# Flamingo layer on one core: values ahead of scores, and the twelve transposes together, in each attention step

## What is computed

```python
# attention (scale = 1/sqrt(sqrt(64)))
x = layer_norm(ctx) ; l = layer_norm(_layernorm(x_in))
q = l @ Wq ; k, v = split(concatenate([x, l]) @ Wkv)
w = softmax((q * scale) @ (k * scale).T)         # 256 x 333 for each head
out = (w @ v).reshape(B, 256, 1024) @ Wo
x_in = x_in + tanh(g_xattn) * out
# then: x + tanh(g_ffn) * (routed experts, top 2 of 16, + a shared expert with a causal conv of 3 taps)
```

## Time and profile before

| | |
|---|---|
| median of 3 runs | 1342.59 us (1341.72 to 1343.8) |
| the profiled execution | 1342.28 us |
| its span, first to last instruction | 1340.5 us |
| TensorE busy | 1251.8 us, 93% |
| VectorE, GpSimd, ScalarE busy | 65%, 55%, 50% |
| mean granted clock of TensorE | 0.988 |

### The profile page before, as it was taken

How to read it: one execution, slowest core, us unless ns; L and a number is a source line. 1 busy time by engine, 2 the same in 40 slices (tenths; PEclk the granted TensorE clock), 3 DMA queues, 4 the chain that set the end, 5 groups by cost and what they waited for, 6 DMA issues and landing times.

```text
span 1340.5 us, 28196 instructions
## 1 busy us (share of the span) xinstructions
PE 1251.8 (93%) x8982; PEld 1018.9 (76%) x8982; DVE 877.1 (65%) x2646; ACT 665.2 (50%) x2022; POOL 739.4 (55%) x894
## 2 busy tenths in 40 slices
PE   1799999999999999999999999999999979999996
PEld 1687888878887878787878787888788867887774
DVE  4567667777776777777777776777776654444454
ACT  2455555455545455455454554555545545444443
POOL 1655555656565666566656655665665522444554
PEclk9999999999999999999999999999999989999998
DMA  4960000000000000000000000000000151445656
GB/s 128 287 181 4 4 1 4 17 4 17 4 18 5 17 4 18 5 17 4 18 6 17 8 13 6 17 11 9 10 9 9 52 149 39 121 127 169 206 177 205
DMA packets 61823, 70.90 MB, mean 53 GB/s; under 512 B 7056, under 2 KB 56160, under 8 KB 61664
## 3 DMA queue, kind: packets, MB, share of 16 engines
q1 hardware_dynamic: 54464, 49.96, 12.9%
q0 software_dynamic: 6912, 18.95, 4.0%
q10 hardware_dynamic: 288, 0.00, 0.0%
HBM read 35.19 MB, written 33.70 MB: 51 GB/s over the span
## 4 chain that ended last, share of the span: by engine, by line
PE 39%; POOL 28%; issue 23%; DVE 5%; DMA 3%; ACT 2%; POOLq 0%; SPq 0%; DVEq 0%; ACTq 0%
POOL probs L1107 19%; PE pj L1344 9%; PE st L560 6%; PE ov L1409 4%; PE st L1390 4%; PE st L1374 3%; POOL probs L1104 3%; POOL slots_x L977 3%; PE pj L513 3%; PE ov L579 3%; PE yb L1470 2%; PE st L550 2%; POOL rstd L1087 1%; DMA slots_x<-h_send,slot_i 1%; DVE PT L1328 1%
## 5 line engine op out<-in xcount | busy, mean ns | idle before, releaser
L1107 POOL TENSOR_SCALAR probs<-probs,inv_sum 128x333 f32<-128x333 f32 x384 | 425.4, 1123 | 0.0
L1157 ACT ACTIVATE probs<-st,neg_max 128x333 f32<-128x333 f32 x512 | 268.5, 537 | 270.9 <-DVE neg_max L1296 270.9
L1104 POOL TENSOR_TENSOR probs<-probs,inv_sum 128x333 f32<-128x333 f32 x128 | 94.7, 740 | 403.2 <-DVE inv_sum L1307 402.9
L1296 DVE TENSOR_REDUCE neg_max<-st 128x2 f32<-128x666 f32 x256 | 205.8, 845 | 133.0 <-PE st L1390 133.0
L1374 PE MATMUL st<-ident,probs 128*128 128x128 f32 (+1 forms) x1536 | 203.8, 272 | 1.1 <-POOL probs L1107 1.1
L1409 PE MATMUL ov<-PT,V 128*64 128x256 f32 (+1 forms) x1536 | 197.1, 392 | 0.0
L1374 PEld LDWEIGHTS st<-ident,probs 128*128 128x128 f32 (+1 forms) x1536 | 182.5, 143 | 17.7 <-POOL probs L1107 1.4
L1344 PE MATMUL pj<-wkv,lT 128*128 128x512 f32 (+1 forms) x576 | 158.4, 410 | 16.3 <-DVE Q_hl L1316 15.8
L1390 PE MATMUL st<-K_hl,Q_hl 64*128 64x334 f32 x1536 | 152.9, 331 | 18.3 <-issue 8.9
L1328 DVE COPY PT<-st 128x512 f32<-128x512 f32 x256 | 163.7, 681 | 0.7 <-PE st L1374 0.7
L1183 ACT ACTIVATE V<-pj 128x512 f32<-128x512 f32 (+1 forms) x96 | 57.2, 596 | 194.4 <-PE pj L1344 194.4
(11 more groups left out here) (174 smaller groups left out, 1729.4 us busy)
## 6 DMA issues: line engine op xcount, KB each, us to landing
slots_x<-zeros SPq DMA_DIRECT2D x10, 1032.0 KB, 13.2
V<-slots_x SPq DMA_DIRECT2D x80, 129.0 KB
yg<-routed_y SPq DMA_DIRECT2D x32, 256.0 KB
out<-X SPq DMA_DIRECT2D x32, 128.0 KB
stage<-in_L_xattn_Wkv SPq DMA_DIRECT2D x4, 512.0 KB, 4.0
X<-in_x SPq DMA_DIRECT2D x2, 1024.0 KB, 14.2
w_gu<-in_L_ffn_expert_gate_w SPq DMA_DIRECT2D x2, 960.0 KB, 9.2
w_gu<-in_L_ffn_expert_up_w SPq DMA_DIRECT2D x2, 960.0 KB, 10.2
```

The source lines that it names most:

```text
L1104: pool.tensor_tensor(probs[:, v, 0, 0:SKV], probs[:, v, 0, 0:SKV], inv_sum[:, v, 0:1].to_broadcast([P, SKV]), ALU.mult).then_inc(normed, 1)
L1107: pool.tensor_scalar(probs[:, v, i, 0:SKV], probs[:, v, i, 0:SKV], inv_sum[:, v, i:i + 1], None, ALU.mult).then_inc(normed, 1)
L1157: nc.scalar.activation(probs[:, v, i, 0:SKV], st_bank(i)[:, 0:SKV], ACT.Exp, bias=neg_max[:, v, i:i + 1], accum_out=sums[:, v, i:i + 1]).t ...
L1296: nc.vector.tensor_reduce(neg_max[:, v, 2 * i:2 * i + 2], st[i][:, :, 0:SKV], AX.X, ALU.max, negate=True).then_inc(maxed, 1)
```

## The change

TensorE: the products with values go ahead of the scores; the twelve transposes, before in two groups (eight ahead of V, four behind it), go together behind V and L in a step with V, ahead of the output projection, and behind the output projection in a step without V. ScalarE copies `ov` to `OT_hl` ahead of the exponentials, and VectorE takes the remainder of `OT_hl` ahead of the maxima (behind the add of a finished batch at p = 3). The routing products stay with the output projection. All waits are the same.

In the diff the blocks of `OT_hl` are shown at their new places only, and of TensorE's the new functions; its block of scores stands behind that of values. `project_out` holds the wait for `ot_lo`, the conv transposes, `route_tensor` and the output projection as they were.

```diff
@@ scalar, step @@
+            if has(LAG_AV):
+                m, v = PAIRS * bb + u - LAG_AV, (u - LAG_AV) % 2
+                act.wait_ge(ov_full, m + 1)
+                if known(m - 1):
+                    act.wait_ge(y_full, m - 1)
+                copy(OT_hl[:, v, 0, :], ov[:, 0:SQ], ACT.Copy).then_inc(ot_hi, 1)
             if has(LAG_S):
...
@@ vector, step @@
+            if has(LAG_AV):
+                m, v = PAIRS * bb + u - LAG_AV, (u - LAG_AV) % 2
+                dve.wait_ge(ot_hi, m + 1)
+                tt(OT_hl[:, v, 1, :], ov[:, 0:SQ], OT_hl[:, v, 0, :].bitcast(F32), ALU.subtract
+                   ).then_inc(ot_lo, 1)
             if has(LAG_S):
...
@@ tensor, step @@
-            if has(LAG_T):
-                pe.wait_ge(normed, 4 * (PAIRS * bb + u - LAG_T + 1))
-                turned(0)
-                turned(1)
             if p in V_STEPS and has(0):
...
-            if has(LAG_T):
-                turned(2)
             if p in L_STEPS and exists(b + 1) and exists(b):
                 transposes(bb, u // PAIRS + 1, L_STEPS[p])
...
+            def turn_probs():
+                if has(LAG_T):
+                    pe.wait_ge(normed, 4 * (PAIRS * bb + u - LAG_T + 1))
+                    turned(0)
+                    turned(1)
+                    turned(2)
+
+            def project_out():
+...
+
+            if p in V_STEPS:
+                turn_probs()
+                project_out()
+            else:
+                project_out()
+                turn_probs()
```

More of the change, by code:

```diff
@@ L1159, in step @@
                                          accum_out=sums[:, v, i:i + 1]).then_inc(exped, 1)
[L1160 to L1165, removed]
             if has(0):
@@ L1307, in step @@
                 nc.vector.reciprocal(inv_sum[:, v, :], sums[:, v, :]).then_inc(inv_ready, 1)
[L1308 to L1312, removed]
             if has(0):
@@ L1375, in turned @@
                 last.then_inc(pt_full, 1)
[L1377 to L1392, removed]
             if has(LAG_AV):
@@ L1411, in step @@
                 last.then_inc(ov_full, 1)
+            if has(LAG_S):
+                m, r = PAIRS * bb + u - LAG_S, (u - LAG_S) % 2
+                _, _, kfree, kvalue = filled("K", PAIRS, bb, u - LAG_S)
+                pe.wait_ge(kfree, kvalue + 1)
+                if known(m):
+                    pe.wait_ge(exped, 4 * m)
+                if known(m - 1):
+                    pe.wait_ge(pt_lo, 2 * (m - 1))
+                    pe.wait_ge(pt_hi, m - 1)
+                for qt in range(QT):
+                    for n, (a, a_) in enumerate(((0, 0), (0, 1), (1, 0))):
+                        for head in range(2):
+                            own = slice(head * HALF, (head + 1) * HALF)
+                            last = mm(st_bank(2 * qt + head)[:, 0:SKVE], Q_hl[own, r, a, qt * P:(qt + 1) * P],
+                                      K_hl[own, r, a_, :], start=(n == 0), stop=(n == 2))
+                    last.then_inc(st_full, 1)
             if has(0):
@@ new lines, in project_out @@
+            def project_out():
+                if has(LAG_Y):
+                    pe.wait_ge(ot_lo, PAIRS * bb + u - LAG_Y + 1)
+                if turns_conv:
+                    if u == 6:
+                        pe.wait_ge(kept.conv_in, 16)
+                    else:
+                        pe.wait_ge(kept.cv_ready, u - 6)
+                    for k in range(KD):
+                        last = nc.tensor.transpose(H_COLS[:, k * P:(k + 1) * P], conv_raw[:, k * P:(k + 1) * P, u - 6], ident[:])
+                    last.then_inc(cv_full, 1)
+                if isinstance(bb, int) and bb == 0 and u == 15:
+                    pe.wait_ge(kept.cv_ready, kept.KS_)
+                    pe.wait_ge(kept.misc_in, 16 * 4)
+                    pe.wait_ge(kept.route_consts, 12)
+                route_tensor(pe, bb, u, has)
+                if has(LAG_Y):
+                    m, v, q = PAIRS * bb + u - LAG_Y, (u - LAG_Y) % 2, (u - LAG_Y) % PAIRS
+                    if q == 0 and known(bb + (u - LAG_Y) // PAIRS):
+                        pe.wait_ge(y_read, bb + (u - LAG_Y) // PAIRS)
+                    if isinstance(m, int) and m == 0:
+                        pe.wait_ge(wo_split, 2)
+                    for t in range(QT):
+                        for i, (a, r_) in enumerate(((0, 0), (0, 1), (1, 0))):
+                            last = mm(yb[:, t * D:(t + 1) * D], OT_hl[:, v, a, t * P:(t + 1) * P], wo[:, r_, q, :],
+                                      start=(q == 0 and t == 0 and i == 0), stop=(q == PAIRS - 1 and i == 2),
+                                      skip_group_check=True)
+                    last.then_inc(y_full, 1)
```

## The result

The changed kernel takes 1601.5 us (median; 1595.5 to 1608.4) against 1343.2 for the kernel before: ratio 1.193, 95% interval 1.188 to 1.197. It is slower by 258 us; 1615 us was predicted. The execution that was profiled is the slowest of the four, 1608.4 us, with a span of 1606.7.

What follows compares the result with a forecast made beforehand. It took TensorE, busy 93%, to bound the kernel, with 4.90 us of chain against 5.10 of cover. 192 + 34 - 10 = 216 us on 1342.3 gave 1558; the clock's 58 gave 1616; predicted 1615, range 1550 to 1690.

Steps and rivals of the forecast that it cites:

- The balance: Scores to V: a 4.90 us chain against 5.10 us of TensorE work, of which the change leaves 2.86.
- Steps with V: The 96 steps with a values projection: each 2.0 us longer, 192 us in all.
- the one behind V: After V in those steps: nothing new waits, so nothing was added; 0.2 us a step left to the upper end.
- Steps without V: The 32 steps p = 3 and 7: values products wait for PT copies, mean 1.05 us each, 34 us in all.
- The clock: TensorE after the new stalls: half of 96 bring the lower clock level, at 1.2 us each, 58 us.
- The four turns of the loop: Turns of the rolled loop, where TensorE idles 2.0 to 2.7 us: two of four were followed by the lower clock.
- The sum: Whole kernel: 216 us added without the clock gives 1558 us; with the clock's 58 us, 1616.
- (a): Rival for the whole kernel: the same stalls, but the clock holds, 1558 us; chance 0.28.
- (b): Rival for the whole kernel: the same stalls, with the lower clock level after each, 1712 us; chance 0.12.
- (c): Rival: not slower, as Q's bank is free in time and V starts as K ends, about 1300 us; chance 0.04.
- (d): Rival: a smaller stall, as the moved pieces cover it elsewhere, half of 216, about 1450 us; chance 0.06.
- What would show it: Signs in the changed profile: Q_hl wait some 200 us, V steps 10 to 11 us, TensorE about 80%, slow clock stretches.

Runs made afterwards that it cites:

- e1: The changed kernel with the transposes put back at their old places (eight ahead of V, four behind): 1477.8 us, ratio 1.102 to the kernel before.
- e3: The changed kernel with the Q projection done three times over ahead of K in each step with V: 1565.0 us, ratio 1.166.
- e4: The changed kernel with Q's high half behind the first exponential on ScalarE and its low half right behind VectorE's maxima: 1433.6 us, ratio 1.068.
- e6: The changed kernel with the twelve transposes ahead of the output projection at p = 3 and 7 too: 1601.0 us, ratio 1.192.
- e12: The changed kernel with the Q projection done twice at p = 0, 1, 2 and 6 only: 1566.9 us, ratio 1.169.
- e11: e5 with VectorE's wait for the first scatter of routed rows moved from ahead of Q_hl to behind the PT copies: 1327.4 us, ratio 0.989.
- e5: The kernel before with Q's high half between the third and fourth exponential and its low half ahead of the reciprocals: 1341.7 us, ratio 1.000.
- e9: The changed kernel with the OT_hl work of ScalarE and VectorE back behind the exponentials and the reciprocals: 1671.1 us, ratio 1.244.
- e8: The kernel before with the Q projection ahead of the values products, and Q's halves taken as in e4: 1354.5 us, ratio 1.009.
- e7: e1 with the edit of e4 (Q's high half behind the first exponential, low half behind the maxima): 1402.7 us, ratio 1.047.

## Why the prediction was right

**The balance.** The chain is what runs from the scores to the read of Q's bank on the other engines; the cover is the work that TensorE has in hand meanwhile. That the step stands on 4.90 us of chain against 5.10 of cover, and that the change takes cover and not chain, is shown by e1 and e3 (cover put back or other work in its place, V stays) and by e4 (chain cut, V follows). Predicted distances to V were 4.83 (p = 4) and 5.70 (p = 2); measured 4.72 and 5.59. For p = 4 the step was predicted at 10.10 and is 10.19.

**Steps with V.** Predicted +2.0 each. With the clock's share out (e3), they are 10.39, 10.55, 11.24, 10.20, 10.20 and 10.80 against 8.33, 8.14, 8.69, 8.15, 8.28 and 8.89: +2.15 in the mean, 206 us in 96 steps in place of 192. The term that came out too low is the one behind V, where I took nothing and left 0.2 open. V starts 0.32 sooner after the scores than before in the mean (medians of e3; the 2.0 has 0.24 in it), and behind V 0.23 a step is lost. At p = 4 and 5 it is 0.2: the twelve transposes end later and ScalarE's PT copy with them (225.36 - 224.34 = 1.02 from the output projection to the values products, where 0.88 lay between it and the scores before). At p = 1 and 2 it is 0.35 and 0.5: there the values products also wait for ScalarE's copy of routing rows out of the bank `ov` (L987, 5.5 us in 20 waits in e3), which the prediction doesn't have.

**Steps without V.** Predicted +0.8 (p = 3) and +1.3 (p = 7), 1.05 in the mean; +0.86 and +0.96 measured. At p = 7 the PT copies on VectorE are what is late, and not the transposes, as e6 shows. At p = 3 the prediction gave its 0.8 no working; the values products wait there for ScalarE's PT copy, and without that for VectorE's read of the logits (e6).

**The clock.** Predicted 58 us, from half of 96 stalls at 1.2 us. Measured by e3 and e12 it is 36 and 35 us. The mis-sized factor is the share: 29 of 94, not a half, while the price, estimated as 36 / 29 = 1.2 us, is as taken. The stalls were put at 2.0 to 2.8 us and are 1.0 to 2.65. The four turns of the loop from which I took the half all idled 2.0 us or more; 43 of the new waits were of 1.8 us or less, and none of those was slow.

**The sum.** Without the clock 1558 was predicted and e3 gives 1565; with it 1616 and 1601.5. The errors of +7 and -22 partly cancel, so part of the total's closeness is luck; that of the steps without the clock isn't, as each kind of step was measured by itself.

**The rivals.** (a), the clock holds, is refuted by e3 and e12. (b), the lower level after every stall, doesn't hold here: 29 of 94. The Trainium skill's page "TensorE: Matmul & The Clock Gate", section "HAM oscillation — how this bites in real kernels", tells of every round of its loop starting cold, that is at half clock; that kernel's waits are of some 3 to 5 us by the page, so what it says of every round is said of longer waits than these of 1.0 to 2.65, and isn't a rule for them. (c) and (d) are refuted by the time. (c) had a point all the same: with Q's bank read sooner and the scatter's wait out of the way (e11) there is something to gain, but 15 us and not 42, and in the old order. Its 42 us were too much from the start, as the 34.5 of the earlier trace rows counts weight loads too; the products alone waited 15.8 us.

**What would show it.** V's wait of some 200 us in about 100 waits: 189 in 96 for the products alone; in the source view, which the prediction named, it is 397.6 in 191. V steps of 10 to 11 us: 10.2 to 11.2 in e3, but 11.8 to 12.4 at p = 0, 2 and 6 in the changed kernel, the clock's share included. TensorE at about 80%: 82%. Slow stretches all through the attention: yes, 0.95 over two rounds.

## What to carry to other kernels

Work of an in-order engine that stands between a producer and the instruction that waits for its result's reader is cover, and the profile shows no wait while it is long enough. Before moving it, follow the waiting instruction's releaser back through the other engines' queues to the instruction that starts the chain, and compare the two lengths; here they were 4.90 and 5.10 us, in 96 steps. The idle time that a line shows can count weight loads and products both: take the products' from the list of waits. If the cover must go, move the reader forward in its own queue first (e4), and look at what else stands behind the next wait in that queue (e5 and e11).

## What the runs showed of the hardware

- In the changed kernel idle stretches of TensorE of up to 1.8 us ahead of V were followed by no slow rows (0 of 43, and 0 of 42 in e6), those of 1.83 to 2.65 us by slow rows in 29 of 51. That is no fixed border: in e9 only 2 of 58 stretches of 1.92 to 2.2 us were, and in e12 one of 1.80 us was. Adding 52 us (e12) or 157 us (e3) of products whose results aren't used made the kernel 35 us faster.
- The same products take TensorE 5.10 us in the order scores, values, Q, K, transposes and 5.29 in the order scores, Q, values, K, transposes (e8): 0.09 more from Q's start to what follows it, and 0.10 more for K. The cause wasn't tried.
- Left open: in the loop of e7 the eight mean step lengths add up to 70.0 us and the medians to 68.6, in the kernel before to 65.8 and 64.8. Turns of the loop are in the means of both; the difference wasn't taken apart.
